# Row order of the stacked q and k operands, and the shape of the transfers that load them

## The chip, the cores and the metric

The kernel runs on one core of a Trainium2 chip. The time is the device time of one execution in microseconds (us). A core has five engines that are programmed apart: TensorE (PE, with its weight loads shown as PEld), VectorE (DVE), ScalarE (ACT), GpSimd (POOL) and SyncE (SP), which here only issues DMA transfers. Sixteen DMA engines move the data. Engines wait for each other by semaphores.

## The reference

Four layers run one after the other over x of shape (32 batches, 256 tokens, 128 features), all in float32, each on a normalized input and added to it: attention A, eight grouped dense layers, attention B, the dense layers again. What the change touches are the score products of both attentions, with 16 heads of 8 dimensions:

```python
# attention A, per batch; q, k: (256 tokens, 16 heads, 8)
score = softmax(einsum('bihd,bjhd->bhij', q, k), axis=-1)
out   = einsum('bhij,bjrd->bihrd', score, v)
# attention B, per batch, per segment of 64 tokens, with a causal mask
scores = matmul(q, swapaxes(k, -2, -1)) / sqrt(8)
A_dot  = matmul(softmax(scores), v)
# and a memory carried from segment to segment:
A_mem = matmul(sigma(q), M) / (sigma(q) @ z);  M += sigma(k)^T (v - V_prev)
```

## The kernel before

One program runs three functions, each with its own loop over the 32 batches: `attention_a` (tiles named a_), `dense` (b_) and `attention_b` (c_). Each is a software pipeline: in body n, batch n is projected and split, batch n-1 gets its scores, batches n-2 and n-3 are finished. Each engine's instruction list is written out by hand in the body (`s` counts 16 steps in `attention_a`, 8 in `attention_b`); nothing is scheduled automatically.

**How a score product is made of bf16 parts.** q and k in float32 are split by POOL into three bf16 parts each (high, middle, low: lines 357 to 360 and 1413 to 1416). The product of two such sums has nine terms, part a of q times part b of k. All nine are done by one matmul whose contraction runs over 9 x 8 = 72 rows: nine pairs of parts, 8 dimensions each. So q is laid out in 72 partitions of the tile `q_st`, and k in 72 of `k_st`, where every part appears three times. The order of the 72 rows is free, so long as q and k have the same.

**How the stack gets there.** The parts are written to DRAM (`parts_dram`, three parts of q and three of k, each of 128 rows ordered dimension, head), by the transfer at line 280 (1339). SP then waits for its completion and issues eight transfers, four for each half of the heads. In the kernel before, q's come first: one for each part, from 8 rows of DRAM that are read three times, into 24 partitions (line 294; 1327). Then one for k: 24 rows read three times, into 72 partitions (line 297; 1331). A row is 8 heads x 256 tokens x 2 bytes = 4 KB. The semaphore `stack_in` counts the four of a half.

**Who waits for it.** In `attention_a`, PE starts body n+1 (step s = 0) with two score units of batch n (`score_half`, line 547) and waits there for `stack_in` of the first half; the second half is needed at s = 6. In `attention_b` the first unit (line 1572) stands at s = 1 and the third, which needs the second half, at s = 4. Before SP overwrites a stack it waits until the matmuls of batch n-2 that read it (`shifted`, lines 562 and 1552) are done.

**The loop around it.** In `attention_a` batch n's stack depends on PE's own body n: its q and k projections stand at s = 3 (lines 616, 617), ACT copies them at s = 4 (453, 455), POOL splits them, the parts go out and come back as the stack. DVE takes the row maxima of the scores (line 666, 1760), splits them (681 to 684), and they come back by PE (608), ACT (446, 464) and POOL (335) as further rows of `q_st`, which line 562 uses to make the scores again with the maximum taken off. ACT exponentiates them (472), and PE multiplies by the values (578).

Of the kernel before, what the change touches and what calls it, by code (L numbers as in the profile page):

```python
# [20 lines left out]
NB, T = 32, 256  # L21
NT = T // P
H, HD, R, QK = 16, 8, 8, 32
RD = R * HD
NPART = 3
SROWS = NPART * NPART * HD
# [36 lines left out]
def apart(eng, spare):  # L63

    eng.sem_inc(spare, 1)


def memory(nc, ctx, prefix):
# [10 lines left out]
def attention_a(nc, d):  # L79
# [6 lines left out]
    with ctx:  # L86
# [42 lines left out]
        parts = [sb(f"a_parts{i}", [P, 2, NPART, T], BF16) for i in range(2)]  # L129
        q_st = [sb(f"a_q_st{i}", [P, H, T], BF16) for i in range(2)]  # L130
        k_st = [sb(f"a_k_st{i}", [P, H, T], BF16) for i in range(2)]
# [52 lines left out]
        stack_in = [[sem(f"a_stack_in{i}{k}") for k in range(2)] for i in range(2)]  # L184
# [19 lines left out]
        parts_dram = d["a_parts_dram"]  # L204
# [13 lines left out]
        def _(sp):  # L218
# [33 lines left out]
            def body(j, u):  # L252
                n = 2 * j + u
                i = u
# [27 lines left out]
                if active(j, u, 0):  # L282
                    sp.wait_ge(parts_out, (n + 1) * 16)
                    apart(sp, spare)
                    if isinstance(j, int) and n < 2:
                        sp.wait_ge(zeros_d, 2 * (n + 1))

                    for half_ in range(2):
                        hs = slice(half_ * H // 2, (half_ + 1) * H // 2)
                        if not isinstance(j, int) or n >= 2:  # L290
                            sp.wait_ge(shifted, (n - 2) * H + (half_ + 1) * H // 2)
                            apart(sp, spare)
                        for a in range(NPART):
                            sp.dma_start(q_st[i][a * NPART * HD:(a + 1) * NPART * HD, hs, :],
                                         parts_dram[i, a].rearrange("(d h) t -> d h t", d=HD)[:, hs].unsqueeze(0)
                                         .broadcast_to([NPART, HD, H // 2, T])).then_inc(stack_in[i][half_], 16)
                        sp.dma_start(k_st[i][0:SROWS, hs, :],
                                     parts_dram[i, NPART:2 * NPART].rearrange("c (d h) t -> (c d) h t", d=HD)[:, hs]
                                     .unsqueeze(0).broadcast_to([NPART, NPART * HD, H // 2, T])
                                     ).then_inc(stack_in[i][half_], 16)  # L300
                if active(j, u, 4):
                    at = pair(j, u, 4)
                    sp.wait_ge(ao_d, (n - 3) * NT)
# [839 lines left out]
def attention_b(nc, d):  # L1143

    ctx = ExitStack()
    with ctx:
# [111 lines left out]
        parts_dram = d["c_parts_dram"]  # L1258
# [19 lines left out]
        def _(sp):  # L1278
# [9 lines left out]
            def body(j, u):  # L1288
# [31 lines left out]
                def stack(h2):  # L1320

                    hs = slice(h2 * H // 2, (h2 + 1) * H // 2)
                    if later(j, n, 2):
                        sp.wait_ge(shifted, (n - 2) * ST + (h2 + 1) * ST // 2)
                        apart(sp, spare)
                    for a in range(NPART):
                        sp.dma_start(q_st[i][a * NPART * HD:(a + 1) * NPART * HD, hs, :],  # L1327
                                     parts_dram[i, NPART + a].rearrange("(d h) t -> d h t", d=HD)[:, hs]
                                     .unsqueeze(0).broadcast_to([NPART, HD, H // 2, T])
                                     ).then_inc(stack_in[i][h2], 16)  # L1330
                    sp.dma_start(k_st[i][0:SROWS, hs, :],
                                 parts_dram[i, 0:NPART].rearrange("c (d h) t -> (c d) h t", d=HD)[:, hs]
                                 .unsqueeze(0).broadcast_to([NPART, NPART * HD, H // 2, T])
                                 ).then_inc(stack_in[i][h2], 16)

                if active(j, u, 0):
                    sp.wait_ge(split_d, (n + 1) * SPLIT)
# [632 lines left out]
```

## Time and profile before

| | us |
|---|---|
| median of 3 runs | 1937.64 |
| lowest, highest | 1916.83, 1940.32 |
| the profiled execution, its span from first to last instruction | 1922.6 |
| of it, `attention_a` (first stack load 21.4, last score matmul 884.4) | about 0 to 930 |
| `dense` | about 930 to 1125 |
| `attention_b` | about 1125 to 1922 |

The profile is that of one execution; for it the page gives the span and no other time. PE is busy for 81% of the span, DVE 75%, POOL 45%, ACT 40%. The mean granted TensorE clock is 0.899 of full speed. The hardware-driven DMA queue carries all 157 MB, and its packets take 24.7% of the time of 16 engines.

How to read it: busy shares say which engine is nearest to its limit, the list of waits says for whom PE stood still, and the timeline of a single body says what those waits are worth. "PEclk" is the granted TensorE clock (1.00 is 2.4 GHz, 0.50 is 1.2 GHz). "DMA share" is the mean busy share of the core's 16 DMA engines in a window.

### The profile page before, as it was taken

Reading aid. Unit: us, or ns where it says so; the run is one execution under the profiler, and the core shown is the slowest. Engines: PE = TensorE matmul, PEld = TensorE weight load, DVE = VectorE, ACT = ScalarE, POOL = GpSimd, SP = SyncE. Lnnn points to the kernel's source line nnn. Section 1 sums busy time; section 2 is a strip of 40 time slices with the busy share of each in tenths; the row PEclk is TensorE's granted clock in tenths of the full one; section 3 lists DMA queues with packets and bytes.
Section 4 is the critical chain, followed back from the end, with each engine's and each line's share of the span. In section 5 each row is a group of like instructions: output and inputs, shape, how many; then the busy total and the mean of one; then the engine's idle time right before and its main releaser. Section 6 shows DMA issues by size and latency. Waiting matters only on the chain. (4 is left out here: it accounts for less than half of the span.)

```text
span 1922.6 us, 45960 instructions
## 1 busy us (share of the span) xinstructions
PE 1565.6 (81%) x13604; PEld 1346.2 (70%) x13668; DVE 1446.9 (75%) x3554; ACT 767.5 (40%) x1731; POOL 866.4 (45%) x1116
## 2 busy tenths in 40 slices
PE   5998988898888988887566645888888888888887
PEld 3988888888888888887355524666666666666665
DVE  5587878887788878876588855777778777777774
ACT  1555555555555555554122221333333333333331
POOL 4355555554555555554455542333343333333331
PEclk8999999999999999999699876999899888898896
DMA  4422122212222222210333212223222222222221
GB/s 122 133 98 77 63 71 82 74 64 74 74 77 71 71 76 74 76 66 21 109 94 99 82 52 77 91 95 100 96 91 96 88 87 88 87 93 87 89 86 37
DMA packets 178621, 158.08 MB, mean 82 GB/s; under 512 B 9457, under 2 KB 160113, under 8 KB 178546
## 3 DMA queue, kind: packets, MB, share of 16 engines
q1 hardware_dynamic: 178546, 157.16, 24.7%
q8 instruction: 38, 0.62, 0.1%
q14 instruction: 37, 0.30, 0.1%
HBM read 113.09 MB, written 44.04 MB: 82 GB/s over the span
## 5 line engine op out<-in xcount | busy, mean ns | idle before, releaser
L578 PE MATMUL a_bank<-a_vp,a_prob 128*128 128x96 f32 x4096 | 662.0, 268 | 0.0
L578 PEld LDWEIGHTS a_bank<-a_vp,a_prob 128*128 128x128 f32 x4096 | 638.4, 200 | 8.2
L666 DVE TENSOR_REDUCE a_nmax<-a_bank 128x2 f32<-128x512 f32 x512 | 347.2, 684 | 158.7 <-PE a_bank L547 157.4
L472 ACT ACTIVATE a_prob<-a_bank 128x512 f32<-128x512 f32 x512 | 306.0, 598 | 359.1 <-PE a_bank L562 358.2
L547 PE MATMUL a_bank<-a_k_st,a_q_st 96*128 96x256 bf16 x1024 | 272.3, 291 | 98.0 <-DMA a_k_st<-scratch_a_parts_dram 90.8
L562 PE MATMUL a_bank<-a_q_st,a_k_st 120*128 120x256 bf16 x1024 | 289.7, 283 | 2.7 <-POOL a_q_st L335 2.7
L335 POOL TENSOR_SCALAR a_q_st<-a_mt 24x2048 bf16<-24x2048 bf16 x64 | 121.4, 1896 | 245.2 <-PE a_bank L562 138.2
L1760 DVE TENSOR_REDUCE c_nmax<-c_bank 128x4 f32<-128x512 f32 x256 | 167.4, 684 | 53.2 <-PE c_bank L1572 51.7
L1602 PE MATMUL c_o_bank<-c_vb,c_prob 128*128 128x96 f32 x1024 | 182.3, 304 | 30.1 <-DVE c_ad L1885 29.2
L547 PEld LDWEIGHTS a_bank<-a_k_st,a_q_st 96*128 96x128 bf16 x1024 | 122.5, 124 | 113.9 <-issue 76.3
L1476 ACT ACTIVATE c_prob<-c_bank 128x256 f32<-128x256 f32 x256 | 98.8, 386 | 200.6 <-PE c_bank L1552 199.0
L1602 PEld LDWEIGHTS c_o_bank<-c_vb,c_prob 128*128 128x128 f32 x1024 | 146.7, 206 | 41.4 <-DVE c_ad L1885 29.1
L392 POOL TENSOR_TENSOR a_prod<-a_ov,a_wgt 128x512 f32<-128x512 f32 x128 | 151.7, 1185 | 37.8 <-POOL a_prod L392 17.1
L1572 PE MATMUL c_bank<-c_k_st,c_q_st 128*128 128x128 bf16 x1024 | 115.2, 243 | 27.0 <-DMA c_k_st<-scratch_c_parts_dram 13.4
L562 PEld LDWEIGHTS a_bank<-a_q_st,a_k_st 120*128 120x128 bf16 x1024 | 127.3, 124 | 12.6 <-issue 5.4
L1572 PEld LDWEIGHTS c_bank<-c_k_st,c_q_st 128*128 128x128 bf16 x1024 | 91.9, 111 | 42.5 <-issue 21.1
L1395 POOL TENSOR_SCALAR c_vb<-c_vs 64x128 f32<-64x128 f32 x128 | 38.7, 302 | 164.6 <-PE c_o_bank L1602 124.9
L1413 POOL TENSOR_SCALAR c_parts<-c_kq 128x512 bf16<-128x512 f32 x32 | 19.8, 618 | 191.4 <-ACT c_kq L1499 191.4
L481 ACT COPY a_ov<-a_bank 128x292 f32<-128x292 f32 x256 | 101.7, 397 | 1.4 <-PE a_bank L578 1.4
L1552 PEld LDWEIGHTS c_bank<-c_q_st,c_k_st 128*64 128x64 bf16 x2048 | 56.1, 117 | 56.4 <-issue 48.3
L1631 PE MATMUL c_bank<-c_uv,c_skn 128*128 128x144 f32 x192 | 46.2, 324 | 57.3 <-DVE c_uv L1797 57.3
L1569 PE MATMUL c_bank<-c_causal,c_ident 128*128 128x512 bf16 x192 | 85.8, 447 | 0.0
(200 smaller groups left out, 3059.6 us busy)
## 6 DMA issues: line engine op xcount, KB each, us to landing
a_q_st<-scratch_a_parts_dram SPq DMA_DIRECT2D x192, 96.0 KB
a_k_st<-scratch_a_parts_dram SPq DMA_DIRECT2D x64, 288.0 KB
c_q_st<-scratch_c_parts_dram SPq DMA_DIRECT2D x192, 96.0 KB
c_k_st<-scratch_c_parts_dram SPq DMA_DIRECT2D x64, 288.0 KB
scratch_a_parts_dram<-a_parts SPq DMA_DIRECT2D x32, 384.0 KB, 2.7
scratch_c_parts_dram<-c_parts SPq DMA_DIRECT2D x32, 384.0 KB, 2.7
a_x<-in_x SPq DMA_DIRECT2D x32, 128.0 KB, 11.3
scratch_y<-a_y SPq DMA_DIRECT2D x32, 128.0 KB, 10.8
```

The lines of the kernel that those rows point to most:

```text
L335: pool.tensor_scalar(q_st[o][MROW:AROWS, hs, :], mt[half_][MROW:AROWS, :].unsqueeze(1).broadcast_to([AROWS - MROW, H // 2, T]), 1.0, 0.0, ...
L392: pool.tensor_tensor(prod[o][:, gs, :].rearrange("p g (e r) -> p g e r", r=R), ov[o][:, gs, 0:RD].rearrange("p g (e r) -> p g e r", r=R), ...
L472: act.activation(prob[h % 4][:, :, :].rearrange("p a b -> p (a b)"), t_ps[h % 2][:, :], ACT.Exp).then_inc(exped, 1)
L481: act.copy(ov[(i + lag) % 2][:, 4 * g:4 * g + 4, :], o_ps[g % 2][:, 0:4 * VC].rearrange("p (g c) -> p g c", g=4)[:, :, 0:CQ]).then_inc(ov_ ...
L547: mm = pe.matmul(s_ps[t][:, hh * T:(hh + 1) * T], q_st[o][0:MROW, 2 * g + hh, t * P:(t + 1) * P], k_st[o][0:MROW, 2 * g + hh, :], start=Tr ...
L562: mm = pe.matmul(t_ps[h % 2][:, c * T:(c + 1) * T], k_st[o][0:AROWS, h, c * P:(c + 1) * P], q_st[o][0:AROWS, h, :], start=True, stop=True)
L578: mm = pe.matmul(o_ps[g % 2][:, at:at + VC], prob[h % 4][:, c, t * P:(t + 1) * P], vp[o][:, c, :], start=c == 0, stop=c == NT - 1)
L666: dve.tensor_reduce(nmax[:, t, 2 * g:2 * g + 2], s_ps[t][:, :].rearrange("p (h k) -> p h k", h=2), AX.X, ALU.max, negate=True).then_inc(ma ...
L1476: act.activation(prob[g % 4][:, :], t_ps, ACT.Exp).then_inc(exped, 1)
L1572: mm = pe.matmul(s_ps[t][:, c * P:(c + 1) * P], q_st[o][:, h, ts], k_st[o][:, h, ts], start=False, stop=True, skip_group_check=True)
L1602: mm = pe.matmul(o_ps[:, t, at:at + WIN], prob[g % 4][:, t * P:(t + 1) * P], vb[st][:, t, at:at + WIN], start=True, stop=True)
L1760: dve.tensor_reduce(nmax[:, t, 4 * q:4 * q + 4], s_ps[t][:, :].rearrange("p (h k) -> p h k", h=4), AX.X, ALU.max, negate=True).then_inc(ma ...
```

## The change

The 72 rows are ordered (part of q, dimension, part of k) instead of (part of q, part of k, dimension). The q side, where each row of DRAM now fills three neighbouring partitions, is loaded by one transfer a half, into all 72 partitions. The k side is loaded by three, one for each part of q, each from 8 dimensions x 3 parts into 24 partitions. Bytes, rows of 4 KB (144 a half), the number of transfers, their semaphore and all waits are the same. In `attention_b` the same is done with q and k at the places that they have there.

```diff
+def left(parts, hs):
+    rows = parts.rearrange("a (d h) t -> (a d) h t", d=HD)[:, hs, :].rearrange("r h t -> r (h t)")
+    return rows.unsqueeze(1).broadcast_to([NPART * HD, NPART, (hs.stop - hs.start) * T])
+
+def right(parts, hs):
+    return parts.rearrange("b (d h) t -> d b h t", d=HD)[:, :, hs, :].rearrange("d b h t -> d b (h t)")
...
+                        sp.dma_start(q_st[i][0:SROWS, hs, :], left(parts_dram[i, 0:NPART], hs)
+                                     ).then_inc(stack_in[i][half_], 16)
                         for a in range(NPART):
-                            sp.dma_start(q_st[i][a * NPART * HD:(a + 1) * NPART * HD, hs, :],
-                                         parts_dram[i, a].rearrange("(d h) t -> d h t", d=HD)[:, hs].unsqueeze(0)
-                                         .broadcast_to([NPART, HD, H // 2, T])).then_inc(stack_in[i][half_], 16)
-                        sp.dma_start(k_st[i][0:SROWS, hs, :],
-                                     parts_dram[i, NPART:2 * NPART].rearrange("c (d h) t -> (c d) h t", d=HD)[:, hs]
-                                     .unsqueeze(0).broadcast_to([NPART, NPART * HD, H // 2, T])
-                                     ).then_inc(stack_in[i][half_], 16)
+                            sp.dma_start(k_st[i][a * NPART * HD:(a + 1) * NPART * HD, hs, :],
+                                         right(parts_dram[i, NPART:2 * NPART], hs)
+                                         ).then_inc(stack_in[i][half_], 16)
...
```

The same edit stands in `stack` of `attention_b`. As the built programs carry them, the patterns are these (count of each dimension, slowest first, and its step in elements of DRAM):

```
          from, before             from, after                 into, before   into, after
q side    3 (step 0) x 8 x 2048    24 x 3 (step 0) x 2048      24 x 2048      72 x 2048
k side    3 (step 0) x 24 x 2048   8 x 3 (step 32768) x 2048   72 x 2048      24 x 2048
```

On SP, in the loop body of `attention_a`, from the store of the parts to the next body's load of x. Each row is a line, an instruction, its tiles, the partitions and elements written, and a count. Before:

```order
L280 DMA scratch_a_parts_dram<-a_parts 128x6x256
L283 REGISTER_ALU
L291 ISA
L294 DMA a_q_st<-scratch_a_parts_dram 24x1x2048 x3
L297 DMA a_k_st<-scratch_a_parts_dram 72x1x2048
L291 REGISTER_ALU
L294 DMA a_q_st<-scratch_a_parts_dram 24x1x2048 x3
L297 DMA a_k_st<-scratch_a_parts_dram 72x1x2048
```

And now:

```order
L291 DMA scratch_a_parts_dram<-a_parts 128x6x256
L294 REGISTER_ALU
L302 ISA
L304 DMA a_q_st<-scratch_a_parts_dram 72x1x2048
L307 DMA a_k_st<-scratch_a_parts_dram 24x1x2048 x3
L302 REGISTER_ALU
L304 DMA a_q_st<-scratch_a_parts_dram 72x1x2048
L307 DMA a_k_st<-scratch_a_parts_dram 24x1x2048 x3
```

Nothing moves past anything else on SP: four transfers a half as before, where three small and one large become one large and three small. No other engine's list changes.

## Rows read from the trace of the kernel before

**Rows 1.** The page, busy time by engine: us (share of the span) xinstructions.
```profile
PE 1565.6 (81%) x13604; PEld 1346.2 (70%) x13668; DVE 1446.9 (75%) x3554; ACT 767.5 (40%) x1731; POOL 866.4 (45%) x1116
```

**Rows 2.** Waits of PE: who waited for whom, us in total, times, longest us.
```profile
PE a_bank L547 <- DMA a_k_st<-scratch_a_parts_dram: 90.8, 30, 6.4
...
PE c_bank L1631 <- DVE c_uv L1797: 57.3, 32, 4.0
PE c_o_bank L1602 <- DVE c_ad L1885: 29.2, 30, 1.3
...
PE c_bank L1572 <- DMA c_k_st<-scratch_c_parts_dram: 13.4, 6, 10.0
```

**Rows 3.** Two windows, projections alone (L616, then L1652; two a batch): PE, PEld, clock, DMA share.
```profile
118.00:845.70 727.70, 16.85 (x54) 8.20 (x54) 0.94 0.21 74
...
1238.00:1859.20 621.20, 16.06 (x54) 8.44 (x54) 0.90 0.27 91
```

**Rows 4.** PE's timeline, one body of attention A and the next one's start: start us, us.
```profile
328.45 0.39 PE L547 MATMUL a_bank<-a_k_st,a_q_st 96*128 96x256 bf16 x2 [2.95 <-DMA a_k_st<-scratch_a_parts_dram]
...
350.99 0.36 PE L578 MATMUL a_bank<-a_vp,a_prob 128*128 128x96 f32 x2
354.26 0.60 PE L547 MATMUL a_bank<-a_k_st,a_q_st 96*128 96x256 bf16 x2 [2.91 <-DMA a_k_st<-scratch_a_parts_dram]
```

**Rows 5.** SP's timeline in that body: the issues of the first half's transfers.
```profile
343.55 2.22 SPq L294 DMA_DIRECT2D a_q_st<-scratch_a_parts_dram  x3
345.82 0.69 SPq L297 DMA_DIRECT2D a_k_st<-scratch_a_parts_dram  x1
```

**Rows 6.** Three windows: us, PE, PEld, DVE, ACT, POOL busy, clock, DMA share, GB/s.
```profile
400.00:403.50 3.50, 3.50 (x37) 3.50 (x36) 3.50 (x6) 2.11 (x6) 2.98 (x3) 1.00 0.19 69
411.50:415.00 3.50, 3.50 (x29) 3.21 (x28) 2.83 (x8) 2.30 (x5) 1.28 (x1) 0.91 0.19 78
422.50:424.50 2.00, 1.78 (x19) 1.62 (x18) 1.97 (x6) 0.92 (x2) 1.30 (x4) 1.00 0.61 197
```

**Rows 7.** DMA issues: count, KB each, median us from issue to landing where given.
```profile
a_q_st<-scratch_a_parts_dram SPq DMA_DIRECT2D x192, 96.0 KB
a_k_st<-scratch_a_parts_dram SPq DMA_DIRECT2D x64, 288.0 KB
...
scratch_a_parts_dram<-a_parts SPq DMA_DIRECT2D x32, 384.0 KB, 2.7
...
a_w_q<-in_a_Wq SPq DMA_DIRECT2D x1, 64.0 KB, 2.0
```

**Rows 8.** Tiles a_k_st and a_q_st: how long SP takes to issue one, ns min/median/max.
```profile
L297 SPq DMA_DIRECT2D a_k_st<-scratch_a_parts_dram x64: 687/688/692, 23.7 to 859.9; - x64
...
L294 SPq DMA_DIRECT2D a_q_st<-scratch_a_parts_dram x192: 678/683/845, 21.4 to 859.2; - x192
```

**Rows 9.** The body of rows 4 as a window, columns as in rows 6.
```profile
328.45:351.00 22.55, 22.26 (x205) 21.17 (x206) 21.22 (x39) 13.62 (x31) 13.43 (x15) 1.00 0.18 63
```

**Rows 10.** PE's timeline, another body: its start, a later pair, its end; and two windows.
```profile
408.83 0.60 PE L547 MATMUL a_bank<-a_k_st,a_q_st 96*128 96x256 bf16 x2 [3.31 <-DMA a_k_st<-scratch_a_parts_dram]
...
432.58 0.36 PE L578 MATMUL a_bank<-a_vp,a_prob 128*128 128x96 f32 x2
...
410.00:412.00 2.00, 2.00 (x12) 1.92 (x11) 1.93 (x6) 0.13 (x1) 0.00 (x0) 0.50 0.18 74
412.00:414.00 2.00, 2.00 (x19) 1.78 (x18) 1.39 (x3) 1.65 (x5) 0.28 (x1) 0.97 0.20 80
```

**Rows 11.** DVE's timeline between the body of rows 4 and the next.
```profile
352.36 0.17 DVE L684 TENSOR_TENSOR a_mpart<-a_nrest,a_mpart 128x16 bf16<-128x16 f32 x1
354.99 0.69 DVE L666 TENSOR_REDUCE a_nmax<-a_bank 128x2 f32<-128x512 f32 x1 [2.46 <-PE a_bank L547]
```

**Rows 12.** Attention B, one body: SP's first stack issue, and PE's first score matmuls of it.
```profile
1401.35 2.22 SPq L1327 DMA_DIRECT2D c_q_st<-scratch_c_parts_dram  x3
...
1412.85 0.39 PE L1572 MATMUL c_bank<-c_k_st,c_q_st 128*128 128x128 bf16 x4 [0.16 <-issue]
```

**Rows 13.** PE's timeline, the first waits for a stack in each attention.
```profile
32.03 1.03 PE L547 MATMUL a_bank<-a_k_st,a_q_st 96*128 96x256 bf16 x4 [6.40 <-DMA a_k_st<-scratch_a_parts_dram]
...
1162.72 0.63 PE L1572 MATMUL c_bank<-c_k_st,c_q_st 128*128 128x128 bf16 x4 [9.97 <-DMA c_k_st<-scratch_c_parts_dram]
```

More of the change, by code:

```diff
@@ L1325, in stack @@
                         apart(sp, spare)
+                    sp.dma_start(q_st[i][0:SROWS, hs, :], left(parts_dram[i, NPART:2 * NPART], hs)
+                                 ).then_inc(stack_in[i][h2], 16)
                     for a in range(NPART):
[L1327 to L1334, printed above, removed]
+                        sp.dma_start(k_st[i][a * NPART * HD:(a + 1) * NPART * HD, hs, :],
+                                     right(parts_dram[i, 0:NPART], hs)).then_inc(stack_in[i][h2], 16)
                 if active(j, u, 0):
```

## The prediction, made before the changed kernel was run

> **What bounds the kernel now.** I read the busy shares first. PE is busy for 81% of the span and DVE for 75% [rows 1]: neither is full, so the 357 us in which PE does nothing are the place to look. The list of PE's waits says for whom it stood. The longest entry is the stack of attention A, 90.8 us in 30 waits, and every other entry of attention A is small. In attention B PE waits for DVE, 57.3 and 29.2 us, and only 13.4 us for its stack [rows 2]. So the transfers that the change reshapes are what stops PE in one of the three stages, and hardly in the others.
>
> Then the timeline of one body of attention A. It starts at 328.45, PE works without a break until 350.99 + 0.36 = 351.35, and the next body starts at 354.26 after a wait of 2.91 for the stack [rows 4]. A body is 22.90 us of PE's work and 2.9 us of waiting. A projection pair is seen once a batch: 54 matmuls in 727.70 us are 27 bodies, 26.95 us each [rows 3].
>
> The missing 1.15 us are the clock. After a wait of 3.31 us PE's granted clock is 0.50 (1.2 GHz) in 410 to 412, and 0.97 in the next 2 us. That body takes 432.58 + 0.36 - 408.83 = 24.11 us, against 22.90 in the body of rows 4, whose clock was 1.00 throughout [rows 4, 9, 10]. So a wait costs its own 2.9 us, and most times 1.2 us more behind it. 22.9 + 1.2 + 2.9 = 27.0, the period found.
>
> **Why the stack is late.** The first transfer of a half is issued at 343.55, PE gets its stack at 354.26, 10.71 us later [rows 4, 5]. While nothing but stack transfers is in flight, the DMA share is 0.19 of 16 engines, that is 3 engines, both in a stretch of q transfers (400 to 403.5) and in one of the k transfer (411.5 to 415). The store of the parts, from 128 partitions, has 0.61 even over a window that it only partly fills [rows 6]. A half is 3 x 96 + 288 = 576 KB [rows 7], and 590 kB at the 78 GB/s of rows 6 take 7.56 us. The other 10.71 - 7.56 = 3.15 us are the start of the first and the completion of the last.
>
> What do the 24-partition and the 72-partition transfer have in common, so that both get three engines? Not where they go, but that the pattern they read begins with the threefold repeat. The change takes that from the front: q now starts with 24 rows, k with 8. That is an inference from two kinds of transfer. The Trainium skill ("DMA: Bandwidth & Descriptors", section "Why a DMA increments its semaphore by 16 and not by 1") states the rule itself: a transfer gets the largest number of engines up to 16 that divides the slowest dimension of both patterns. By it, 3 before for both, with which the share of 0.19 agrees, and after the change 12 for q and 8 for k; no run so far shows those two.
>
> **What the change does to it, step by step.** With e engines at the rate of one (78 / 3 = 26 GB/s), a half lands about 3.15 + 22.7/e us after the first issue. It can't land before the last of four issues of 0.68 to 0.69 us [rows 8] has ended (2.9 us) and that one has completed, for which 2.0 us is the nearest row, a 64 KB load [rows 7]: 4.8 us at best. At worst nothing changes, 10.7 us.
>
> Between those ends the exact value hardly matters, and this is the point of the forecast. In the body at full clock the first issue came at 343.55 and PE's work ended at 351.35: PE can do without its stack for 7.8 us [rows 4, 5]. 3.15 + 22.7/e is below 7.8 from e = 5 on; with 4 engines a wait of 1.0 us would be left. I take the case of 5 or more. By the page's 12 and 8 a half would land after some 5.5 us, an estimate, and the sum would be the same.
>
> The removed wait is then gone whole, and with it the idle stretch before which the clock always fell. **Attention A: 26.95 - 22.90 = 4.05 us a body.** What is late next? DVE. It is busy for 21.22 of that body's 22.55 us [rows 9], and finishes the maxima of the old body at 352.53, 1.2 us after PE is done [rows 11]. PE's first score unit of the next body doesn't need it, and a unit takes 0.7 us until DVE could start, so DVE would begin some 0.5 us late, with 1.3 us to spare over the body. I allow 0.1 us and take a period of 23.0. Of the 30 waits, 28 are in full bodies: 28 x 3.95 = 111 us.
>
> The first wait of attention A is 6.40 us [rows 13]. Landing can be 10.7 - 5.5 = 5 us earlier; but weight loads fill the engines at that time, so I take 3, and 1 for the second. **Attention A, beginning: 4 us.**
>
> **Attention B.** Its period is 621.20 / 27 = 23.0 us [rows 3]. The first issue is at 1401.35 and PE uses that stack at 1412.85, 11.5 us later, without a wait [rows 12]: 10.7 fits. The transfer is hidden in nearly all bodies, and an earlier landing moves nothing there: PE's waits for DVE stay. Only the beginning is exposed, 9.97 us of the 13.4 [rows 2, 13]; 5 of it go, and 2 of the rest. **7 us.**
>
> The issue costs nothing new: four a half before and after, and 24 and 72 partitions cost SP the same 0.68 and 0.69 us [rows 8]. The loads of x and the stores of y, which queue behind the stack on the same three engines, land earlier; nobody was seen waiting for them, so nothing comes of it. PE's matmuls read as many rows as before.
>
> **Sum: 111 + 4 + 7 = 122 us.** The profiled span of 1922.6 becomes about 1801. The median of the runs, 1937.64, is 15 above that span, and the three runs lie 23 us apart, so I can't say in which of them the next ones will be: with 122 off the median and off the span I get 1816 and 1801, and put **1812 us**.
>
> **The rivals.**
>
> *DVE takes over in attention A.* For it: only 1.3 us are left in a body, and its work overlaps the body's end. Against it: in the body of rows 4 PE never stood still for DVE. If PE then had to wait until DVE is done with the old body, 1.2 us each (22.9 + 1.2 = 24.1), the gain would be 28 x 2.85 = 80 plus 11: 1937 - 91, about 1847 us. 13%.
>
> *The engine count stays at 3*, because something other than the leading repeat sets it, such as the threefold dimension wherever it stands (it is still there, second). Then only the order of the four issues differs, and the time is 1938, give or take 15. For it: I have only two kinds of transfer, both with three engines. 6%.
>
> *Fewer engines than 3 (slower).* The mechanism: the number is found by another property of the two patterns, and for the new ones it comes out as 2 or 1. It decides from e = 2 on: a half lands after 3.15 + 11.35 = 14.5 us, 3.8 later than now, which PE in attention A waits for in full (32 x 3.8 = 122), and in attention B beyond its 11.5 (32 x 3.0 = 96): 2156 us. With one engine the 45 us for both halves would exceed a body and the time go beyond 3000. Against it: 24 and 8 have more divisors than 3. 4%.
>
> *More than I count, from attention B.* The clock there is at half speed a fifth of the time (0.90 in rows 3), after waits for DVE. If loads landing earlier shifted its bodies so that the waits shrank and half the clock loss went, a further 30 us would: 1780. Nothing shows that they would. 5%.
>
> **How the numbers follow.** My forecast has 72%, and its own range is 1790 to 1835: 23 us between runs, and the beginnings of both loops, which I only estimate. The range 1780 to 1855 takes in the DVE rival and the better case and leaves out the two rivals at and above the old time, and the tails of mine. A run-to-run difference of 2% is about what can be told from no change, 39 us. Faster by more than that: 72 + 13 + 5, or 90%. Within it 6%, slower 4%.
>
> **What would show it.** In the profile after: the DMA share where only the stack is in flight rises from 0.19 to 0.5 or more, and the stretch shortens to 2 or 3 us a half. If it stays 0.19, the cause that I infer is wrong. PE's wait for the stack in attention A falls from 90.8 us to under 10; the period of L616 to about 23; the clock there from 0.94 to 1.00. If instead PE waits at L547 or L608 for DVE, the first rival holds. The period of L1652 in attention B stays within 1 us of 23.0; if it doesn't, my claim that the transfer is hidden there is wrong.

## The result, and the profile after

| | before, us | after, us |
|---|---|---|
| median of 4 runs | 1933.32 (1916.83 to 1940.32) | 1807.01 (1797.48 to 1813.6) |
| ratio | | 0.9356, 95% interval 0.931 to 0.9401 |
| span of the profiled execution | 1922.6 | 1799.0 |
| mean granted TensorE clock | 0.899 | 0.929 |

The forecast was 1812 us from 122 us less in the profiled execution; it is 123.6 us less. That sum is right for a partly wrong reason, as the stages show.

Each kernel below was timed beside runs of the kernel before made at the same time, and its ratio is to the fast ones of these; their medians lie at 1920 to 1926 us, so the ratios and the bodies in the traces compare better than the microseconds.

The page's busy shares, for [rows 1]:

```profile
PE 1516.6 (84%) x13604; PEld 1309.6 (73%) x13668; DVE 1456.8 (81%) x3554; ACT 767.1 (43%) x1731; POOL 866.8 (48%) x1116
```

PE's waits, for [rows 2]. Columns: who waited for whom, us in total, times, longest.

```profile
PE c_bank L1636 <- DVE c_uv L1802: 57.2, 32, 3.9
PE a_bank L556 <- DVE a_nmax L675: 35.4, 82, 1.5
PE c_o_bank L1607 <- DVE c_ad L1890: 29.2, 30, 1.3
...
PE c_bank L1577 <- DMA c_k_st<-scratch_c_parts_dram: 6.6, 1, 6.6
...
PE a_bank L556 <- DMA a_k_st<-scratch_a_parts_dram: 2.2, 1, 2.2
```

The wait of 90.8 us for attention A's stack is down to a single 2.2, and the one of 13.4 in attention B to a single 6.6, at the loop's beginning. New in its place stands a wait for DVE's row maxima, 35.4 us in 82 pieces.

Windows over the steady part of attention A and of attention B, 27 bodies each, for [rows 3]. Columns: window, its length, busy time of PE, PEld, DVE, ACT and POOL, granted clock, DMA share, GB/s.

```profile
112.10:751.30 639.20, 608.15 (x5566) 576.70 (x5565) 605.18 (x1135) 391.49 (x864) 393.29 (x433) 1.00 0.29 84
...
1131.60:1730.60 599.00, 506.15 (x5133) 399.26 (x5186) 475.32 (x1482) 203.11 (x513) 229.65 (x378) 0.94 0.32 94
```

Attention A's body is now 639.2 / 27 = 23.67 us (26.95 before), attention B's 599.0 / 27 = 22.19 (23.0 before). Cutting both spans at the same places of the program gives where the 123.6 us came from:

| stage | before | after | difference |
|---|---|---|---|
| to the 5th projection of attention A | 116.4 | 112.1 | -4.3 |
| attention A, 27 bodies | 727.7 | 639.2 | -88.5 |
| its end, dense, start of attention B | 297.7 | 293.6 | -4.1 |
| attention B, first 4 bodies | 94.1 | 86.7 | -7.4 |
| attention B, 27 bodies | 621.2 | 599.0 | -22.2 |
| the rest | 65.4 | 68.4 | +3.0 |

The shape of the transfers. SP's issues for the first half of one batch's stack, and two short windows in which nothing but that stack is in flight, the first with a q transfer, the second with k ones:

```profile
406.60 0.82 SPq L304 DMA_DIRECT2D a_q_st<-scratch_a_parts_dram  x1
407.48 2.06 SPq L307 DMA_DIRECT2D a_k_st<-scratch_a_parts_dram  x3
```
```profile
408.20:408.90 0.70, 0.70 (x9) 0.70 (x8) 0.70 (x2) 0.47 (x1) 0.70 (x1) 1.00 0.71 246
412.60:413.60 1.00, 1.00 (x12) 1.00 (x10) 0.88 (x2) 0.82 (x3) 0.82 (x2) 1.00 0.50 143
```

Where three engines' worth, 0.19, stood in [rows 6], there is 0.71 for q and 0.50 for k. 12 of 16 are 0.75, 8 of 16 are 0.50. The stretch shortens as well: this body moves 176 GB/s from 408.0 to 411.4, 598 kB or about one half of the stack, where 590 kB took 7.56 us by the rate of [rows 6].

PE's timeline over the start of the next body:

```profile
414.24 0.38 PE L556 MATMUL a_bank<-a_k_st,a_q_st 96*128 96x256 bf16 x2
...
416.39 0.28 PE L556 MATMUL a_bank<-a_k_st,a_q_st 96*128 96x256 bf16 x1 [0.32 <-DVE a_nmax L675]
...
419.09 0.39 PE L556 MATMUL a_bank<-a_k_st,a_q_st 96*128 96x256 bf16 x2 [0.57 <-DVE a_nmax L675]
```

The stack is first used at 414.24 without a wait, 7.6 us after its first issue; I had put PE's budget at 7.8. The waits that came are short and lie at the third score unit and beyond, where PE needs one of the two score banks back that DVE hasn't read yet.

### The profile page after: what moved, and what is told of

Its sections match the earlier page's. It is cut to its first block and busy times, and to the rows that moved or that the text cites. A ratio compares the mean times of both kernels' runs of the same rounds, so it can differ in the third digit from the quotient of the medians.

```text
span 1799.0 us, 45960 instructions
## 1 busy us (share of the span) xinstructions
PE 1516.6 (84%) x13604; PEld 1309.6 (73%) x13668; DVE 1456.8 (81%) x3554; ACT 767.1 (43%) x1731; POOL 866.8 (48%) x1116
## 5 line engine op out<-in xcount | busy, mean ns | idle before, releaser
L587 PE MATMUL a_bank<-a_vp,a_prob 128*128 128x96 f32 x4096 | 635.2, 261 | 0.0
L587 PEld LDWEIGHTS a_bank<-a_vp,a_prob 128*128 128x128 f32 x4096 | 610.6, 192 | 5.6
L556 PE MATMUL a_bank<-a_k_st,a_q_st 96*128 96x256 bf16 x1024 | 260.6, 278 | 38.4 <-DVE a_nmax L675 35.4
L571 PE MATMUL a_bank<-a_q_st,a_k_st 120*128 120x256 bf16 x1024 | 281.7, 276 | 3.2 <-POOL a_q_st L344 3.2
L556 PEld LDWEIGHTS a_bank<-a_k_st,a_q_st 96*128 96x128 bf16 x1024 | 116.2, 118 | 57.5 <-DVE a_nmax L675 53.4
L1577 PE MATMUL c_bank<-c_k_st,c_q_st 128*128 128x128 bf16 x1024 | 108.3, 233 | 19.4 <-issue 10.0
L1577 PEld LDWEIGHTS c_bank<-c_k_st,c_q_st 128*128 128x128 bf16 x1024 | 86.1, 105 | 36.8 <-issue 11.2
L1636 PE MATMUL c_bank<-c_uv,c_skn 128*128 128x144 f32 x192 | 47.1, 329 | 57.2 <-DVE c_uv L1802 57.2
L1557 PE MATMUL c_bank<-c_q_st,c_k_st 128*64 128x64 bf16 x2048 | 84.3, 207 | 0.0
```

What stands on the lines that cost most here:

```text
L556: mm = pe.matmul(s_ps[t][:, hh * T:(hh + 1) * T], q_st[o][0:MROW, 2 * g + hh, t * P:(t + 1) * P], k_st[o][0:MROW, 2 * g + hh, :], start=Tr ...
L571: mm = pe.matmul(t_ps[h % 2][:, c * T:(c + 1) * T], k_st[o][0:AROWS, h, c * P:(c + 1) * P], q_st[o][0:AROWS, h, :], start=True, stop=True)
L587: mm = pe.matmul(o_ps[g % 2][:, at:at + VC], prob[h % 4][:, c, t * P:(t + 1) * P], vp[o][:, c, :], start=c == 0, stop=c == NT - 1)
L1557: mm = pe.matmul(t_ps[hh * SEG:(hh + 1) * SEG, cs], k_st[st][:, 2 * g + hh, cs], q_st[st][:, 2 * g + hh, cs], start=False, stop=True, skip ...
L1577: mm = pe.matmul(s_ps[t][:, c * P:(c + 1) * P], q_st[o][:, h, ts], k_st[o][:, h, ts], start=False, stop=True, skip_group_check=True)
```

## Which part of the change does it

**Attention A alone.** The row order of attention B is put back (shortened; the texts in angle brackets stand for the old patterns).

```diff
 # attention_b, per half
-sp.dma_start(q_st[i][0:SROWS, hs, :], left(parts_dram[i, NPART:2 * NPART], hs))
-for a in range(NPART): sp.dma_start(k_st[i][24 * a:24 * (a + 1), hs, :], right(...))
+for a in range(NPART): sp.dma_start(q_st[i][24 * a:24 * (a + 1), hs, :], <part a, read three times>)
+sp.dma_start(k_st[i][0:SROWS, hs, :], <three parts, read three times>)
```

> Only attention A has the new row order and transfers; attention B is as before. Stage by stage, the two profiles differ by 4 us before the loop of attention A is steady, 88 in its 27 steady bodies (26.95 to 23.67 each), 4 up to attention B and 27 in attention B (7.5 in its first three bodies, 22 in the other 28, whose clock is at half speed 3.4 us less often a body). Theory 1 (B's 22 us are the state that its clock falls into, not the transfers): this kernel has the same chances of either state as any other, so it saves 92 to 100, and up to 20 more when B falls into the short state: 1815 to 1840 us, most likely 1835. Theory 2 (B's 22 us come from B's own transfers landing earlier): B is as before in every run, 1933 - 96 = 1837 us, and in the profile B's steady body stays at 23.0 with 6.8 us at half clock in most bodies.

**Attention B alone.** The same edit, undone in attention A instead.

> Only attention B has the new row order and transfers; attention A is as before. Theory 1 (only B's beginning is exposed to its stack): about 8 us less than before, 1925 us, with runs up to 20 us lower or higher by the clock state. Theory 2 (B's steady bodies gain too): 30 us less, 1903 us in every run, and in the profile a steady body of 22.2 us with 3.4 us at half clock. In both, attention A's body stays at 26.95 us and its DMA share at 0.19 in stretches with stack transfers alone.

A alone: 1831.27 us, ratio 0.9527 (0.9479 to 0.9575). B alone: 1906.99 us, ratio 0.9914 (0.988 to 0.9948). 4.7% and 0.9% make 5.6%, of the whole change's 6.4% (5.99 to 6.9); with their own intervals, half a point and a third, the two reach 6.2 and so meet it. The steady stretches, attention B of the first kernel, and of the second:

```profile
1136.10:1755.20 619.10, 533.85 (x5187) 405.16 (x5186) 478.57 (x1482) 203.07 (x513) 229.41 (x378) 0.91 0.27 92
```
```profile
1227.20:1826.20 599.00, 517.02 (x5187) 399.18 (x5186) 475.35 (x1482) 203.11 (x513) 229.60 (x378) 0.94 0.32 94
```

Each stage follows its own edit: attention A's body is 23.67 us in the first kernel and 26.94 in the second, attention B's 22.93 and 22.19. So attention B gains by its own transfers, though its stack was hidden. How much is less sure than the 22 us of the profiled executions. The ten runs of B alone are 17 us (10 to 23) faster than the kernel before, its loop's beginning included, which by the table above is worth 7; the profiled one is the fastest of the ten.

What is gained is TensorE's clock. In [rows 3] it is 0.90: 2 x 0.10 x 621 = 124 us at half speed; in the window after 0.94: 2 x 0.06 x 599 = 72. Half of those 52 us are 26 us of matmul time, against 22 measured.

A body of attention B comes in three lengths, with the clock. Three bodies of the kernel before, columns as in [rows 6]:

```profile
1324.38:1345.86 21.48, 17.72 (x192) 13.95 (x193) 17.56 (x56) 7.52 (x19) 8.50 (x14) 1.00 0.29 97
1345.86:1368.57 22.71, 19.05 (x192) 14.99 (x193) 17.75 (x56) 7.52 (x19) 8.49 (x14) 0.92 0.28 97
...
1527.37:1551.38 24.01, 20.34 (x193) 15.67 (x194) 17.97 (x56) 7.52 (x19) 8.49 (x14) 0.86 0.25 86
```

Before, 13 of the 27 steady bodies are long ones, like the third; with A alone 12; in the changed kernel and with B alone none. They are most of the 22 us: 13 times the 1.3 us between the second row and the third are 17.

A alone couldn't tell the two theories of its expectation apart, 1835 and 1837 us. B alone could: none of its ten runs is above 1908.9, near the 1903 of theory 2 and below the 1925 of theory 1. The expectation's "most bodies" with 6.8 us at half clock were 12 of 27.

## Why the number of engines rose

I had inferred that the leading repeat cost the engines. Two kernels load other rows for k so that the slowest dimension of what is read is 3, or 2, with no repeat at all. They leave out the right k rows, so their scores are wrong; bytes, partitions and order are those of the changed kernel.

```diff
-    return parts.rearrange("b (d h) t -> d b h t", d=HD)[:, :, hs, :].rearrange("d b h t -> d b (h t)")
+    rows = parts.rearrange("b (d h) t -> (b d) h t", d=HD)[:, hs, :].rearrange("r h t -> r (h t)")
+    return rows.rearrange("(b s d) f -> b s d f", b=3, s=2)[:, 0]   # second kernel: b=2
...
-                                         right(parts_dram[i, NPART:2 * NPART], hs)
+                                         right(parts_dram[i], hs)
```

> As the changed kernel, but each k transfer reads rows in a pattern of 3 x 8 x 2048 elements (step 65536, not zero) instead of 8 x 3 x 2048: the same bytes into the same partitions, from other rows, so the scores are made from other parts. It leaves the right k rows out. Theory 1 (the slowest dimension's size sets the number of engines): k goes back to 3 engines, a DMA share of 0.19 while k alone is in flight; a half takes 0.95 (q) + 3.8 (k) and lands 3.15 + 4.75 = 7.9 us after the first issue, against the 7.6 after which PE starts the next body: a wait of 0.3 us at most, 0 to 15 us in all, 1807 to 1822 us. Theory 2 (only the leading repeat, step zero, confines a transfer): the share stays 0.50 and the time 1807.

> As the run before, but the k transfers read 2 x 12 x 2048 elements. It leaves the right k rows out too. Theory 1 (size of the slowest dimension): 2 engines, share 0.125 with k alone; a half lands after 3.15 + 0.95 + 5.7 = 9.8 us, 2.2 later than PE needs it in attention A, and the clock falls again: 27 x (2.2 + 1.2) less the 0.7 us a body that PE now waits for DVE, 73 us, so about 1880 us. In attention B, with 11.5 us to spare, only its beginning is later, 3 us. Theory 2 (only a repeat confines): 1807 us, share 0.50.

With 3: 1815.74 us, ratio 0.9415 (0.9352 to 0.9477). With 2: 1902.1 us, ratio 0.9875 (0.9798 to 0.9951). A window with k's transfers alone in flight, of the first; three of the second, the first of which holds the end of PE's wait:

```profile
416.00:417.00 1.00, 1.00 (x12) 1.00 (x11) 0.97 (x2) 0.84 (x3) 0.88 (x1) 1.00 0.19 74
```
```profile
428.00:429.00 1.00, 0.46 (x4) 0.45 (x5) 0.00 (x0) 0.00 (x0) 0.00 (x0) 0.91 0.14 54
429.00:430.00 1.00, 1.00 (x7) 0.93 (x7) 0.94 (x2) 0.00 (x0) 0.00 (x0) 0.50 0.14 57
430.00:431.00 1.00, 1.00 (x7) 0.93 (x6) 0.97 (x4) 0.00 (x0) 0.00 (x0) 0.50 0.12 49
```

3/16 = 0.19 and 2/16 = 0.125: the share follows the size of the slowest dimension, and a repeat isn't needed for it to be low. So my reason was too narrow: the repeat cost engines by being three long and standing first. This is what the Trainium skill says ("DMA: Bandwidth & Descriptors", section "Why a DMA increments its semaphore by 16 and not by 1"): the largest number up to 16 that divides both slowest dimensions. All six cases here agree with it: 3, 3 before, 12 and 8 after, 3 and 2 in these.

PE's waits from 120 to 740 us, of the kernel with 3, then of the one with 2:

```profile
PE a_bank L557 <- DMA a_k_st<-scratch_a_parts_dram: 15.6, 25, 1.3
PE a_bank L557 <- DVE a_nmax L676: 13.1, 39, 0.6
```
```profile
PE a_bank L557 <- DMA a_k_st<-scratch_a_parts_dram: 59.5, 23, 4.1
PE a_bank L557 <- DVE a_nmax L676: 4.9, 22, 0.2
```

Two things to see. With 3 the stack is late again by 0.6 us a body, and the body is 23.72 us as against 23.67: the wait for the stack only takes the place of waits for DVE, which fall from 29.9 us in the same stretch of the changed kernel to 13.1. So freeing q alone is nearly enough: with q at 12 engines and k at 3, the ratio of 0.9415 can't be told from the whole change's 0.9356. And with 2 the clock falls again behind the wait (0.91, then 0.50): after a wait of 2.78 us for the stack, at 428.54. The body is 26.30 us. This kernel has the changed kernel's one large and three small transfers in the same order, and differs from it in k's pattern and rows alone: so it is the engines that gain the time in attention A, and not the order of the issues.

## What holds attention A's body at 23.67 us

The forecast was 23.0. First suspicion: the step comp3, which VectorE does in each body. Its line before, and after (duration ns min/median/max):

```profile
L757 DVE TENSOR_TENSOR a_comp<-a_comp,a_cmax x32: 412/415/1711, 88.6 to 905.2; 128x256 f32<-128x256 f32 x32
```
```profile
L766 DVE TENSOR_TENSOR a_comp<-a_comp,a_cmax x32: 424/1273/1710, 84.4 to 809.5; 128x256 f32<-128x256 f32 x32
```

The same step takes 0.86 us more in the median, and 0.63 in the mean of the 27 steady bodies (0.65, then 1.28). The timelines of the kernel after, VectorE, then GpSimd, say beside what:

```profile
418.95 1.27 DVE L766 TENSOR_TENSOR a_comp<-a_comp,a_cmax 128x256 f32<-128x256 f32 x1
```
```profile
418.06 1.90 POOL L344 TENSOR_SCALAR a_q_st<-a_mt 24x2048 bf16<-24x2048 bf16 x1 [2.69 <-PE a_bank L571]
```

GpSimd's step ends at 419.96, VectorE's at 420.22, 0.26 us behind it: started inside the other, it stood until that one was through. In the whole trace 30 of the 32 start so, and all 30 end 0.27 us behind GpSimd's step; before, 7 of 32 did. The Trainium skill describes such a pair ("SBUF — State Buffer", section "Who interferes with whom"): VectorE and GpSimd share a pair of ports as a lock held for a whole instruction, which a VectorE step with two inputs in SBUF needs while GpSimd reads, and a reduction never does. The rows here agree: the sums over the products, reductions that read SBUF, take 1.20 to 1.22 us in all 64 cases, whatever runs beside them.

**The step made later**, where GpSimd is through:

```diff
                 reduces(2, 3)
-                weighs(4, 5)
                 for k in range(MP // 2):
                     ...
+                    if k == 1:
+                        weighs(4, 5)
```

> The changed kernel, with one VectorE step of attention A later in its list: the subtraction of the maximum in the weighing (comp3 = comp2 - cmax) after the next row maximum and the first two moments. In the changed kernel it takes 1.25 us, against 0.69 before, since it is issued while GpSimd writes the maxima into q_st and ends right after that. Theory 1 (VectorE's list bounds the body of 23.67 us, and this step is what stretched it): the step takes 0.42 us, the body 22.9 to 23.0 us, PE's waits for a_nmax fall from 35 to about 15 us, and the kernel saves 18 to 20 us: 1788 us. Theory 2 (PE bounds the body, and its short waits would turn up elsewhere): the step is shorter and the body stays at 23.67, 1807 us.

```profile
L766 DVE TENSOR_TENSOR a_comp<-a_comp,a_cmax x32: 407/408/723, 85.9 to 809.5; 128x256 f32<-128x256 f32 x32
```

The step shrank to 0.41 us as meant, and nothing else moved: 1809.77 us, ratio 0.9407 (0.9383 to 0.9431), body 23.68, and VectorE idle 0.74 us more in each (busy 585.3 us in the 27 bodies, 605.2 before that edit). The theory that VectorE's total sets the body fell.

**VectorE's work cut, and raised.** Cut: half of what the sum over the products reads is left out. Raised: one such sum more, into a tile that nobody uses, in the middle of the body; once on the changed kernel and once on the one before.

```diff
-  prod[o]... "p (h i) (e r) -> p i h e r" [:, t]
+  prod[o]... "p (h i) (e r) -> p i h e r" [:, t, :, :, 0:R // 2]
```
```diff
+  dve.tensor_reduce(extra[...], prod[o]...[:, 0], AX.X, ALU.add).then_inc(extra_d, 1)
   dve.tensor_reduce(ao[o][:, t, :]..., prod[o]...[:, t], AX.X, ALU.add)
```

> The changed kernel, with both sums over the products in attention A taken over half of the products (0.6 us instead of 1.21 each); the other half is left out. Theory 1 (VectorE bounds): 1.2 us less of it a body, which is more than the 0.7 to 1.0 that PE has to give, so the body falls to PE's own 22.7 to 22.9 us: 20 to 26 us less, 1784 us. Theory 2 (PE bounds): no change.

> The changed kernel, with one more sum of 1.21 us in each body of attention A on VectorE, into a tile that nobody reads. Theory 1 (VectorE bounds): the body grows by all of it, 24.9 us, and the kernel by 31 x 1.21 = 37 us at most, 33 in 27 steady bodies: 1840 us. Theory 2 (PE bounds, VectorE has 0.95 us idle a body): at most 0.3 us a body, 8 us.

> The kernel before, with the same additional sum. If the stack was what bounded its body (2.9 us of waiting), VectorE has room at the end of the body: 0 to 0.3 us a body, 0 to 10 us in all, 1926 to 1936 us. If VectorE bounded the body there too, the body grows by 1.2 and the kernel by 33 us.

| | us | ratio to before | attention A's body | VectorE busy in its 27 bodies |
|---|---|---|---|---|
| changed, less | 1790.95 | 0.931 (0.9283 to 0.9338) | 23.03 | 568.6 (605.2) |
| changed, more | 1809.24 | 0.9419 (0.9384 to 0.9453) | 23.68 | 611.6 (605.2) |
| before, more | 1936.15 | 1.0058 (1.0029 to 1.0087) | 26.87 | 599.2 (593.5) |

The last column has in brackets what it is without the edit. On the kernel before, attention A's body had room for 1.2 us, as expected: there the stack was the bound. The kernel as a whole got 0.6% slower, clear of noise; its body of attention A didn't, and where the 11 us come from was not found. On the changed one a cut of 1.07 us gives 0.64, but 1.2 us more cost nothing. A plain full engine would answer alike in both directions. I then thought that only VectorE's list around the body's end counts, ahead of the row maxima for which PE waits, and tried that place from both sides.

**The same extra sum at the body's end**, ahead of the last two row maxima, and **the second of the two sums taken from there** into the middle:

```diff
+  if active(j, u, 4):                                                                    # behind y
+      ...
+      dve.tensor_reduce(extra[...], prod[i]...[:, 0], AX.X, ALU.add).then_inc(extra_d, 1)
```
```diff
-                reduces(6, H // 2)
+                reduces(6, 7)
+                if active(j, u, 4):
+                    summed(1)
+                reduces(7, H // 2)
 ...
-                reduces(12, 13)
-                if active(j, u, 4):
-                    summed(1)
-                reduces(13, 14)
+                reduces(12, 14)
```

> The changed kernel with the same extra sum on VectorE as the seventh run (about 1.2 us a body), but placed behind y, just ahead of the last two row maxima of the body. Theory (VectorE's list around the body's end is what the next body's score units wait for): all of it falls ahead of a_nmax, attention A's body goes from 23.68 to about 24.8 us, 28 x 1.15 = +32 us, 1840 us. Rival (VectorE's steps have room wherever they stand, as in the middle of the body): no change, 1806 to 1812 us, body 23.7.

> The changed kernel with the same VectorE steps in attention A, but one sum over the products (the second one of summed, about 1.2 us) moved from just ahead of the body's end into its middle. Nothing is added or left out. Theory (the place decides, not VectorE's total): the row maxima come earlier by up to that time, body about 23.1 us, 28 x 0.55 = -15 us, 1792 us. Rival (the total decides, or the products' chain through GpSimd does): no change, 1805 to 1812 us.

Both came out nearly as the rival had it. More at the end: 1812.79 us, ratio 0.9464 (0.9387 to 0.9541), body 23.84 against 24.8 expected. Sum moved away: 1817.57 us, ratio 0.9487 (0.943 to 0.9545), body 23.66 against 23.1. The theory of the place fell too. That both kernels as wholes are slower than 1807 is mostly attention B's doing: its unchanged code took 608.0 and 610.6 us in its 27 steady bodies instead of 599.0.

What became of the added 1.2 us a body? They are 32 us over the 27 bodies, yet VectorE is busy for only 6 us more with the sum in the middle (table), and for 4 more with it at the end (608.9): other steps of VectorE got shorter. It can be read off the end of a body. First VectorE and then GpSimd of the changed kernel:

```profile
433.75 1.33 DVE L718 TENSOR_SCALAR a_y<-a_x,a_mv,a_r 128x128 f32<-128x128 f32 x2
...
436.39 1.12 DVE L690 CAST a_mpart<-a_nmax 128x16 bf16<-128x16 f32 x1
437.54 0.17 DVE L691 TENSOR_TENSOR a_nrest<-a_nmax,a_mpart 128x16 f32<-128x16 f32 x1
437.75 1.11 DVE L692 CAST a_mpart<-a_nrest 128x16 bf16<-128x16 f32 x1
```
```profile
431.31 1.90 POOL L344 TENSOR_SCALAR a_q_st<-a_mt 24x2048 bf16<-24x2048 bf16 x1 [0.44 <-POOL a_r L389]
433.55 1.18 POOL L401 TENSOR_TENSOR a_prod<-a_ov,a_wgt 128x512 f32<-128x512 f32 x1 [0.34 <-DVE a_ao L728]
...
436.28 1.18 POOL L401 TENSOR_TENSOR a_prod<-a_ov,a_wgt 128x512 f32<-128x512 f32 x1 [0.18 <-POOL a_prod L401]
437.65 1.18 POOL L401 TENSOR_TENSOR a_prod<-a_ov,a_wgt 128x512 f32<-128x512 f32 x1 [0.18 <-POOL a_prod L401]
```

and the same two of the kernel with the extra sum late:

```profile
436.62 1.21 DVE L829 TENSOR_REDUCE a_extra<-a_prod 128x128 f32<-128x1024 f32 x1
...
439.14 0.17 DVE L692 CAST a_mpart<-a_nmax 128x16 bf16<-128x16 f32 x1
439.35 1.16 DVE L693 TENSOR_TENSOR a_nrest<-a_nmax,a_mpart 128x16 f32<-128x16 f32 x1
440.55 0.17 DVE L694 CAST a_mpart<-a_nrest 128x16 bf16<-128x16 f32 x1
```
```profile
439.30 1.18 POOL L403 TENSOR_TENSOR a_prod<-a_ov,a_wgt 128x512 f32<-128x512 f32 x1 [0.18 <-POOL a_prod L403]
```

The four steps that split the maxima, 128x16 elements each, take 0.17 us alone, and up to 1.2 us when they start inside one of GpSimd's four products, because such a step stands until that product ends: the cast of 436.39 ends at 437.51, the product of 436.28 at 437.46. All 60 casts of the trace that start inside a product end 0.03 to 0.04 us behind it. In the changed kernel two of the four steps stand. In the other only one does (439.35, beside the product of 439.30), since the extra sum, a reduction, ran through meanwhile, and the cast of 439.14 fell between two products. So VectorE's busy time is partly standing time, and work put in front of the split uses it up.

What these rows don't explain is the 0.7 us between 23.0 and 23.67. The two standing casts of a body's end were there before the change too, 60 in its trace as well, so they didn't come with the shorter body. Nor does work taken away turn into standing time: with both sums halved VectorE's busy time fell by 36.6 us, and the work was 28.8. The products were not moved. Nor was a third score bank tried, the plain rival: PE writes its score units into two banks in turn and waits in 73 short pieces (29.9 us from 120 to 740) for DVE to read them, while DVE in the same stretch waits 12.6 us for PE; neither is full.

The sum moved to the middle doesn't help either. GpSimd's products wait for that sum (0.34 us behind a_ao, at 433.55), but GpSimd itself is busy with a_q_st until 433.21, so they could have begun at most 0.34 us earlier.

**y made by ScalarE.** y, two steps of VectorE at the end of the body (1.4 us), goes to ScalarE, which has most room; its bias takes GpSimd two small steps more. **The three moves together**: y on ScalarE, the comp3 step later, the sum earlier. All of the work is kept in both.

```diff
-                if active(j, u, -1):
-                    for t in range(NT):
-                        normed(t)
 # attention_a, ScalarE, in steps 13 and 14
...
+  act.activation(y[1 - i][:, t, :], x[1 - i][:, t, :], ACT.Identity, scale=r1[:, t:t + 1],
+                 bias=nb[:, t:t + 1]).then_inc(y_d, 1)
 # GpSimd, with what counts these steps raised by two
+  norm(6, pool.tensor_tensor(rt[:, 0, :], mv[:, :, 0], r1[:, :], ALU.mult))
+  norm(7, pool.tensor_scalar(nb[:, :], rt[:, 0, :], -1.0, 0.0, ALU.mult, ALU.add))
```

> The changed kernel with attention A's y (the normed copy of x, 1.45 us on VectorE at the end of each body) made by ScalarE instead, its bias -m*r by two small GpSimd steps more. Theory (VectorE's list around the body's end is the bound): VectorE reaches the next row maxima about 1.4 us earlier, the body falls until TensorE's own 22.7 us and its remaining waits take over, about 22.9 to 23.1 us, 28 x 0.7 = -20 us, 1788 us. Rival (another chain, or ScalarE's, sets the end, since y now waits for GpSimd and ScalarE, and the next body's projections wait for y): 1805 to 1830 us, body 23.7 or longer, with TensorE waiting for y's transfer or transposes.

> The three moves together (y on ScalarE, the step comp3 minus cmax made later, the one sum earlier), all work kept. If VectorE's list at the body's end is the bound, taking more away from it than TensorE's own time asks for gives no more than the floor: body 22.7 to 22.9 us, 28 x 0.85 = -24 us, 1785 us. Rival (the moves meet another bound at the same place, ScalarE's or GpSimd's): no better than the tenth run alone, 1788 to 1800 us.

y on ScalarE: 1766.45 us, ratio 0.9208 (0.9155 to 0.9261). All three: 1762.85 us, ratio 0.9194 (0.914 to 0.9247); both are faster than the changed kernel, and the three moves together by 3.6 us more than y alone, 0.2%, little beyond the spread of their runs. The steady windows, attention A and B, of the first:

```profile
114.40:739.30 624.90, 613.63 (x5564) 578.52 (x5563) 566.40 (x1081) 408.07 (x918) 401.08 (x487) 1.00 0.31 86
1120.80:1701.30 580.50, 499.50 (x5131) 392.97 (x5185) 463.03 (x1482) 203.09 (x513) 230.83 (x378) 0.95 0.34 97
```

and of the second:

```profile
113.80:736.60 622.80, 603.29 (x5565) 576.39 (x5564) 538.57 (x1082) 407.98 (x918) 398.39 (x487) 1.00 0.30 86
1116.20:1694.10 577.90, 496.99 (x5133) 391.38 (x5186) 462.81 (x1482) 203.10 (x513) 230.74 (x378) 0.96 0.34 98
```

Attention A's body is 23.15 us, then 23.07: 14 and 16 us less than the changed kernel over 27 bodies, of 20 and 24 expected. VectorE's busy time falls from 605 to 539 us, and the body stops following: there PE's busy 603 of 623 us is the nearest bound. The other 18 to 21 us of the gain come from attention B, 580.5 and 577.9 instead of 599.0, **whose code is the same**. PE's wait for c_uv there is 45.4 us instead of 57.2, and the granted clock 0.95 and 0.96 instead of 0.94. The short kind of body is 20.3 us there instead of 21.3, and 12 and 13 of the 27 are of it instead of 6. So these two times must not be credited to VectorE's relief alone.

## Why the prediction was right, and where it wasn't

- **The stack was the bound, and its engines the reason.** Right, in size too: share 0.71 and 0.50 instead of 0.19, the 90.8 us gone but for 2.2. The 12 and 8 engines by the Trainium skill's rule ("DMA: Bandwidth & Descriptors", section as above) held. My own reason, the repeat, was too narrow: a slowest dimension of 3 without a repeat gives 0.19 as well.
- **PE's budget of 7.8 us, so that from 5 engines on nothing depends on the number.** Right: 7.6 us measured and no wait. The k side with 3 engines and q with 12 still comes within 0.6 us. The formula behind it, each engine at 26 GB/s, was too fast: q's window has 246 GB/s on 12 engines, k's 143 on 8, which are 20 and 18 an engine. The budget was wide enough for that. The issue, taken as costing the same, takes SP 0.78 us for q's 72 partitions instead of 0.69, which the budget hid too.
- **The clock comes back with the wait.** Right: 0.94 to 1.00 in attention A, and 0.50 again behind the wait in the kernel with k at 2 engines. That it "always fell" was too much: the body of [rows 9] ran at 1.00 behind a wait of 2.95 us.
- **28 x 3.95 = 111 us from attention A.** This is the step that failed. 88.5 us in 27 bodies, 3.28 each. The term mis-sized is the next bound: "with 1.3 us to spare over the body. I allow 0.1 us". PE waits for VectorE 1.1 us a body (35.4 us over the loop), in short pieces. The 1.3 us to spare were VectorE's idle time summed over a body, and that was no reserve: a wait arises wherever a maximum comes later than PE needs its bank. One step got longer with the change (comp3), but shortening it again gave nothing; less work on VectorE gave 0.64 and 0.52 us a body. Which step or bank sets the 23.67 stays open. The rival that VectorE takes over had the right engine, and 24.1 us a body was too much.
- **The beginnings, 4 us and 7 us.** Measured 4.3 for attention A, and 7.4 for the first four bodies of attention B. Right in sum; of the wait of 9.97 us 3.4 went, not 5.
- **An earlier landing moves nothing in attention B's steady bodies.** Wrong by 22 us in the profiled executions, though by my own test, the period within 1 us of 23.0, it passed with 22.19. The test was too wide: 27 x 0.8 is 22 us. The rival that named this (30 us, from the clock) had 5%.

88.5 + 22.2 for the two steady loops stands against 107 + 0: the errors of -18 and +22 cancel. That the sum came out within 2 us is luck; that the forecast was near it rests on attention A, where the mechanism held and four fifths of the term came.

**What stays open.** How the landing of attention B's stack reaches PE's clock there. Over nine kernels with the new row order and its 12 and 8 engines, attention B's steady body took 21.40 to 22.62 us; over the three with the old order 22.93 to 23.14; with k at 3 or 2 engines 22.62 and 22.89. The groups stand in order, the first two apart and the third touching the first, but kernels that differ only in attention A differ by 1.2 us in attention B, more than the 0.8 that I read as the change's gain there. The count of long bodies shows why:

| rows of attention B's stack | kernels | long bodies of 27, one profiled execution each |
|---|---|---|
| old order | 3 | 12, 13, 15 |
| new order | 9 | 0, 0, 0, 0, 1, 1, 5, 5, 7 |
| new order, k at 3 and at 2 engines | 2 | 7, 11 |

The long bodies mostly come in runs of four to seven, which some executions fall into and others don't. That faster transfers make them rarer is shown by the two groups, which don't overlap, and by the times of B alone (0.9914, its whole interval below 1); that it is 22 us in general is not. Open too is what holds attention A's body at 23.67: which of GpSimd's or VectorE's steps, or the number of score banks.

## What to carry to other kernels

For a transfer with few engines, look at the slowest dimension of both sides before looking at bytes: the same 590 kB with a slowest dimension of 24 or 8 instead of 3 took an eighth off the body of attention A. When a wait is going to vanish, don't take the next engine's idle time for a reserve, nor its busy time for work: here 32 us of added sums made VectorE busy for only 4 to 6 us more, and its 1.3 us of idle time a body didn't keep PE from waiting 1.1 for it. And cut the two spans by stage before calling a sum right.

## What the runs showed of the hardware that was not expected

- A VectorE step of 128x16 elements took 0.17 us alone and up to 1.2 us beside a product of GpSimd's, ending 0.03 us behind it; one of 128x256 with two inputs 0.42 and 1.27. Reductions stayed at 0.68 and 1.21. So 1.2 us of added reduction cost a body nothing to 0.17 us.
- What an issue costs depends on the pattern, not on the partitions: the q transfer into 72 partitions with the repeat inside took SP 0.78 us in the median, the k transfer into 72 before 0.69 [rows 8].
- The transfers queued behind the stack land much earlier. Issue to landing, of the kernel after; before it was 11.3 and 10.8 us. But for the very first x, nobody in attention A waited for them in either.

```profile
a_x<-in_x SPq DMA_DIRECT2D x32, 128.0 KB, 3.2
scratch_y<-a_y SPq DMA_DIRECT2D x32, 128.0 KB, 2.9
```

- The clock of one stage can change with the code of another: attention B's granted clock was 0.94 in the changed kernel, and between 0.92 and 0.96 in seven kernels where only attention A's code was different. Between the changed kernel and the one with the sum moved, 12 us of attention B (599.0 and 610.6) came from there.
